# Expert stages of a two-block network: each token through its two chosen experts only, sorted by pair

## The reference, cut to what matters

```python
scores = jnp.einsum('bsd,de->bse', x, gate_w) + gate_b      # 4 experts
probs = jax.nn.softmax(scores, axis=-1)
topk_vals, topk_idx = jax.lax.top_k(probs, 2)
mask = jnp.sum(jax.nn.one_hot(topk_idx, 4), axis=-2)
masked = probs * mask
masked = masked / (jnp.sum(masked, axis=-1, keepdims=True) + 1e-09)
h = jax.nn.gelu(jnp.einsum('bsd,edh->ebsh', x, w1) + b1)    # 96 -> 384
y = jnp.einsum('ebsh,ehd->ebsd', h, w2) + b2                # 384 -> 96
out = jnp.einsum('bse,ebsd->bsd', masked, y)
...
t = t + _L0_ffn_ref(_ln_t(t), ...)
```

## Time and profile before

| what | value |
|---|---|
| median of three runs | 2661.78 us |
| span of the profiled execution | 2652.1 us |
| median less span | 9.7 us |
| stage 1 (to about 281 us) | 281 us |
| stage 2, experts (281 to 943) | 662 us |
| stage 3 (943 to 1989) | 1046 us |
| stage 4, experts (1989 to 2652) | 663 us |
| TensorE busy over the span | 89% |

### The profile page before, as it was taken

One profiled execution on the slowest core, in us unless ns is written; L12 is line 12 of the kernel. 1 busy time (PEld: TensorE's weight loads), 2 busy tenths in 40 slices (PEclk: granted clock), 3 DMA queues, 4 the chain that ended last, 5 costly groups with the idle time before them and its releaser, 6 DMA issues.

```text
span 2652.1 us, 72974 instructions
## 1 busy us (share of the span) xinstructions
PE 2365.9 (89%) x26354; PEld 1941.0 (73%) x26354; DVE 2112.4 (80%) x6729; ACT 1423.8 (54%) x2676; POOL 1125.1 (42%) x999
## 2 busy tenths in 40 slices
PE   3665799999999958999899989999968999999998
PEld 2554577777777747888787878888756777777776
DVE  4887788888888757888888878988857888888886
ACT  2332477777777634333333433333316777777776
POOL 1002244444444425555555545555533444444443
PEclk8777799999999978899998888988958999999999
DMA  6000000000000000000000000000000000000001
GB/s 120 1 0 0 16 1 0 0 0 0 0 0 0 1 18 3 3 3 2 4 2 3 2 3 3 2 3 2 3 2 1 0 24 0 0 24 0 24 0 24
DMA packets 39776, 19.48 MB, mean 7 GB/s; under 512 B 38146, under 2 KB 39332, under 8 KB 39560
## 3 DMA queue, kind: packets, MB, share of 16 engines
q1 hardware_dynamic: 39560, 16.43, 3.0%
HBM read 10.13 MB, written 6.29 MB: 6 GB/s over the span
## 4 chain that ended last, share of the span: by engine, by line
PE 63%; issue 19%; POOL 9%; DVE 8%; ACT 1%; POOLq 0%; DVEq 0%; ACTq 0%
PE ps L744 15%; PE ps L745 15%; PE ps L746 15%; PE ps L829 4%; PE ps L763 3%; POOL arena L506 3%; POOL arena L487 2%; PE ps L870 2%; PE ps L890 2%; PE ps L857 1%; PE ps L756 1%; PE ps L874 1%; POOL xn L498 1%; POOL arena L512 1%; DVE arena L939 1%
## 5 line engine op out<-in xcount | busy, mean ns | idle before, releaser
L442 POOL TENSOR_TENSOR rounded<-arena,rounded 128x512 fp32r<-128x512 f32 x384 | 497.2, 1295 | 729.2 <-ACT arena L578 729.2
L744 PE MATMUL ps<-rounded 128*96 128x512 f32 (+3 forms) x1856 | 728.3, 392 | 3.7 <-DVE rounded L366 3.0
L745 PE MATMUL ps<-rounded 128*96 128x512 f32 (+3 forms) x1856 | 698.6, 376 | 0.0
L746 PE MATMUL ps<-rounded 128*96 128x512 f32 (+3 forms) x1856 | 696.0, 376 | 0.0
L577 ACT ACTIVATE rounded<-ps 128x512 fp32r<-128x512 f32 x768 | 459.4, 598 | 317.3 <-PE ps L746 317.1
L578 ACT ACTIVATE arena<-ps 128x512 f32<-128x512 f32 x768 | 456.3, 594 | 0.0
L1203 DVE TENSOR_TENSOR rounded<-arena,rounded 128x512 fp32r<-128x512 f32 x384 | 278.4, 737 | 208.3 <-ACT arena L578 208.3
L829 PE MATMUL ps<-rounded 128*128 128x224 f32 (+1 forms) x2256 | 371.8, 309 | 40.8 <-ACT rounded L607 17.3
L746 PEld LDWEIGHTS ps<-rounded 128*96 128x96 f32 (+2 forms) x1856 | 331.0, 178 | 92.8
L745 PEld LDWEIGHTS ps<-rounded 128*96 128x96 f32 (+2 forms) x1856 | 335.6, 181 | 70.4 <-issue 0.2
L829 PEld LDWEIGHTS ps<-rounded 128*128 128x128 f32 x2256 | 324.2, 210 | 85.3 <-issue 31.7
(11 more groups left out here) (169 smaller groups left out, 3911.3 us busy)
## 6 DMA issues: line engine op xcount, KB each, us to landing
residual<-in_x SPq DMA_DIRECT2D x16, 384.0 KB, 6.3
out<-residual SPq DMA_DIRECT2D x16, 384.0 KB, 5.2
w<-in_w SPq DMA_DIRECT2D x4, 576.0 KB
arena<-in_W_conv SPq DMA_DIRECT2D x1, 756.0 KB
consts<-in_consts SPq DMA_DIRECT2D x1, 280.0 KB, 3.5
arena<-in_W2T SPq DMA_DIRECT2D x16, 4.0 KB
arena<-in_Win_x SPq DMA_DIRECT2D x1, 84.0 KB
arena<-in_Win_z SPq DMA_DIRECT2D x1, 72.0 KB
```

The costliest lines, as they stand in the source:

```text
L442: pool.tensor_tensor(hidr[:, 1, r, :], hid[:, r, :], hidr[:, 0, r, :].bitcast(F32), ALU.subtract).then_inc(f["low_pool"], 1)
L744: pe.matmul(dst, left[0], right[0], start=start, stop=False)
L745: pe.matmul(dst, left[1], right[0], start=False, stop=False)
L746: return pe.matmul(dst, left[0], right[1], start=False, stop=stop)
```

## The change

The expert stages are rewritten (`route` and `expert_tiles` in place of `ffn`), on all engines.

**Routing** (`route`), 4 groups of 4096 tokens. VectorE norms the rows into `stage`, whose row has 196 numbers: x, normed x, two weights, the token's number (`ROW`, `COL_GA`, `COL_GB`, `COL_ID`). ScalarE copies x there. TensorE transposes and computes the gate, plain float32. VectorE ranks, sets one of 6 pairs of experts for each token (`chosen`), TensorE counts the tokens before each one with two matmuls (`strict`, `every`), VectorE makes the slot (`placed`). GpSimd scatters each of 32 image rows with an indirect DMA, 128 rows of 784 bytes, into the DRAM tensor `rows`, where each pair has a region. After the last group VectorE makes a plan of the tiles (`planned`): TILES = (16384 + 6 x 511) // 512 = 37, each of one pair. SP pads the end of each region (`pads`).

**Tiles** (`expert_tiles`), 37 of 512 tokens, 6 chunks each, all unrolled. For each tile SP reads three numbers of the plan into registers (`value_load`) and issues three DMAs at addresses that depend on them: the token rows (512 x 784 bytes) and the split weights of two experts (each 128 x 5384 bytes, into `wring`, 2 slots). The result is added to the token rows in `xs`, and GpSimd scatters it with four indirect DMAs of 128 x 384 bytes: to the DRAM tensor `x1` in stage 2, to the output in stage 4.

**Around them.** The weights are split once, during stage 1, by GpSimd (`expert_parts`, 8 times) and written to DRAM (`wsp`). `xr` is read again from `x1` before stage 3. The output DMAs of SP are gone. Up has three banks in place of two, the lag is 4, GpSimd takes chunks 2 and 5, and the second bias is added by VectorE.

The diff, cut to its core:

```diff
-    def ffn(f, ln_before): ...                       # on each engine, 32 tiles x 12 chunks
+CPT = 2 * CPE
+LAG = 4
+XRING, HIDS, UPS = 6, 3, (0, 1, 5)
+ON_POOL = (2, 5)
...
+            # SP
+            def expert_tiles(l):
+                def tokens(t):
+                    if t >= TILES:
+                        return
+                    if t >= XRING:
+                        sp_.wait_ge(y_out[t % XRING], 16 * Q * uses(l, t - XRING, XRING))
+                    n = sp_.value_load(plan[0:1, 0, t:t + 1], min_val=0, max_val=NPAIR * REGION + (FILL - 1) * T512)
+                    sp_.dma_start(xs[:, t % XRING, :, :], rows[bass.ds(n, T512), :].rearrange("(p q) n -> p q n", q=Q)).then_inc(x_ld[t % XRING], 16)
+                def weights(t, e):
+                    if t >= 2:
+                        sp_.wait_ge(f["y_ev0" if e == 0 else "y_ev1"], l * TILES + t - 1)
+                    n = sp_.value_load(plan[0:1, 1 + e, t:t + 1], min_val=0, max_val=NEXP - 1)
+                    sp_.dma_start(wring[:, t % 2, e, :].bitcast(F32), wsp[l, bass.ds(n, 1), :, :].rearrange("o p n -> (o p) n")).then_inc(w_ld[t % 2][e], 16)
+                tokens(0)
+                for t in range(TILES):
+                    for e in range(2):
+                        weights(t, e)
+                    tokens(t + 1)
...
+            # GpSimd
+            def route(l):
+                def powers(g):
+                    pool.wait_ge(rt["var"], l * G + g + 1)
+                    pool.tensor_tensor(mom2[:, g % 2, 5, :], mom2[:, g % 2, 4, :], half_neg[:, :], ALU.pow).then_inc(rt["rstd"], 1)
+                def scatter(g):
+                    pool.wait_ge(rt["slots"], l * G + g + 1)
+                    pool.wait_ge(rt["copied"], l * G + g + 1)
+                    for h in range(SIDE):
+                        pool.indirect_dma_start(rows, bass.IndirectOffsetOnAxis(ap=slot[:, g % 2, h:h + 1], axis=0), stage[:, g % 2, h, :], None).then_inc(r_out[g % 2], 16)
...
+                powers(0)
+                for g in range(G):
+                    if g + 1 < G:
+                        powers(g + 1)
+                    scatter(g)
+            def expert_tiles(l):
...
+                for step in range(LAST + 3 * CPT):
+                    t, c = divmod(step, CPT)
+                    if c in ON_POOL and step < LAST:
+                        pool.wait_ge(f["gelu"], l * LAST + step + 1)
+                        if step >= CPT:
+                            pool.wait_ge(f["down"], l * LAST + step - CPT + 1)
+                        pool.tensor_tensor(hidr[:, 1, c, :], hid[:, step % HIDS, :], hidr[:, 0, c, :].bitcast(F32), ALU.subtract).then_inc(f["low_pool"], 1)
+                    if c in ON_POOL:
+                        scatter(t - 2, range(0, 2) if c == ON_POOL[0] else range(2, Q))
...
+            # TensorE
+                for step in range(LAST + LAG + 3):
+                    t, c = divmod(step, CPT)
+                    if step < LAST:
+                        up(step)
+                    if LAG <= step < LAST + LAG:
+                        down(step - LAG)
+                    if c == 2 and t + 1 < TILES:
+                        columns(t + 1)
+                    if (due := half_tile(step, LAG + 2)) is not None:
+                        y_rows(*due)
...
+            # VectorE
+            def route(l):
...
+                row_sums(0)
+                for g in range(G):
+                    normed(g)
+                    if g + 1 < G:
+                        row_sums(g + 1)
+                    gated(g)
+                    placed(g)
+                planned()
+            def expert_tiles(l):
...
+                for step in range(LAST + LAG + 4):
+                    t, c = divmod(step, CPT)
+                    if (due := half_tile(step, LAG + 1)) is not None and due[1] == 1:
+                        y_second(due[0])
+                    if (due := half_tile(step, LAG + 3)) is not None:
+                        combine(*due)
+                    if c == 4 and t + 1 < TILES:
+                        columns(t + 1)
+                    if step < LAST and c not in ON_POOL:
+                        dve.wait_ge(f["gelu"], l * LAST + step + 1)
+                        dve.tensor_tensor(hidr[:, 1, c, :], hid[:, step % HIDS, :], hidr[:, 0, c, :].bitcast(F32), ALU.subtract).then_inc(f["low"], 1)
```

More of the change, by code:

```diff
@@ L271, in bank, with uses, half_tile @@
             return ps[:, b:b + n, :].rearrange("p a b -> p (a b)")
[L273 to L279, removed]
+        def uses(l, t, ring):
+            return l * len(range(t % ring, TILES, ring)) + t // ring + 1
+        def half_tile(step, lag):
+            t, e = divmod(step - lag - (CPE - 1), CPT)
+            if e % CPE == 0 and 0 <= t < TILES:
+                return t, e // CPE
+            return None
+        LAST = CPT * TILES
         def layer_norm(dve, ch, src, dst, n, width, which_eps, count, ready, part=None, own=None, rows=None):
@@ new lines, in _ @@
+            sp_.wait_ge(b2_set, 1)
+            for l in range(2):
+                with nc.allow_non_contiguous_dma(reason="biases, one element to a partition"):
+                    sp_.dma_start(b2[0:D, l, :, 0:1], inp["ffn"][l]["b2T"].rearrange("d (e o) -> d e o", o=1)).then_inc(rc_in, 16)
+                sp_.dma_start(gw[0:D, l, :], inp["ffn"][l]["gate_w"]).then_inc(rc_in, 16)
+                sp_.dma_start(gw[D:D + 1, l, :], inp["ffn"][l]["gate_b"]).then_inc(rc_in, 16)
+            raw_weights(0)
@@ new lines, in gates, with expert_tiles, columns @@
+            def gates(l, g, k):
+                pe.wait_ge(rt["xt"], (l * G + g) * NQ + k + 1)
+                if k == 0 and (g or l):
+                    pe.wait_ge(rt["gates"], l * G + g)
+                for i in range(Q):
+                    at_col = (Q * k + i) * NEXP
+                    ins = pe.matmul(bank(5)[:, at_col:at_col + NEXP], xt[0:D + 1, k % 2, i * P:(i + 1) * P], gw[0:D + 1, l, :], start=True, stop=True)
+                ins.then_inc(rt["gate_pe"], 1)
+            def expert_tiles(l):
+                def columns(t):
+                    pe.wait_ge(x_ld[t % XRING], 16 * uses(l, t, XRING))
+                    need(pe, f["x_lo"], l * TILES + t)
@@ L800, in ffn @@
-                pe.wait_ge(f["parts"], 1)
-                tiles(pe, tile)
+                        need(pe, f["y_ev0" if e == 0 else "y_ev1"], l * TILES + t)
+                    mine = [x for x in range(CPT) if (x in ON_POOL) == (c in ON_POOL)]
+                    pe.wait_ge(f["low_pool" if c in ON_POOL else "low"], (l * TILES + t) * len(mine) + mine.index(c) + 1)
+                    w = wring[:, t % 2, e, W1COLS:W1COLS + W2COLS].rearrange("p (s c d) -> p s c d", s=2, d=D)
+                    product(bank(2 + e)[0:D, :], halves(w[:, :, n, :]), halves(hidr[:, :, c, :]), n == 0, n == CPE - 1).then_inc(f["down"], 1)
```

678 lines of the change are left out of this document (421 added, 257 removed).

## The result

The changed kernel took 2714.41 us (median of 4 runs, 2712.84 to 2725.24) beside 2660.92 us before: the ratio is 1.0213, with a 95% interval from 1.0188 to 1.0237. It is slower, clear of the interval; whether by more than 2% the interval leaves open. The forecast was 2579 us and faster.

The account below looks back on a forecast made before the run. TensorE was taken to bound the expert stages, 1324 us. Two stages of 443 + 132X plus a 12 us reload give 898 + 264X, 1241 at X = 1.3: -83, span 2569, median 2579 us; 8-in-10 range 2430 to 2790.

Parts of the forecast that it names:

- A group is 32X + 5.4: Routing: GpSimd's 32 indirect DMAs plus one 5.4 us power set a group's time, binding from X = 0.7 on.
- X: GpSimd's time for one indirect DMA: taken as 1.3 us, ends kept 0.32 and 2.65, break-even 1.61.
- Products: Expert tiles: 222 chunks in place of 384; TensorE takes 9.4 us a tile, 349 us for 37.
- SP's loop: Expert tiles: weights wait for the tile before last, tokens queue behind; at least 10.2 us a tile, taken as 10.0, 370 us.
- Routing, where increments are on time: All work in front of a stage's first product: 61 + 128X, with about 40 us to the first group's slots.
- two round trips: Routing's first group: VectorE's small operations with two round trips to TensorE, together 13 us.
- The ends: Each expert stage: drain 6, slow clock at the start 3, last scatter 4X + 3 us.
- The reload: Between the stages: group 0 of x is read again before stage 3, 12 us, once.
- Rival 1: Indirect DMAs dear, issued serially on GpSimd: 2808 us at X = 2.0, 3173 at 2.65; chance 0.17.
- Rival 2: SP's loop is longer: at 12 us a tile +148, 2727 us; chance 0.13.
- Rival 3: VectorE binds the routing, with X under 1.0: 2405 us at X = 0.32; chance 0.13.
- Rival 4: VectorE's operations hold up GpSimd's issues of indirect DMAs; chance 0.10.

Follow-up runs that it names:

- both: Changed kernel with tokens loaded two tiles ahead and one semaphore increment for a group's 32 statistics: 2550.32 us, 0.96 of before.
- powers_early: Changed kernel with tokens two tiles ahead, one increment per group's statistics, and GpSimd's powers of three groups before its first scatter: 2540.65 us, 0.9574 of before.
- unchanged: The changed kernel run again on another chip, nothing edited: 2606.99 us, 0.9815 of before.
- paced: Changed kernel with each indirect DMA of the routing waiting for the one before to land: 2972.99 us, 1.1178 of before; repeated, 2966.84.
- plain_dma: Changed kernel with SP's plain in-order DMAs in place of the routing's indirect ones, so another output: 2505.12 us, 0.9436 of before; repeated, 2508.11.
- mixed: Changed kernel with plain DMAs in the first routing; in the second, indirect DMAs back to back, one at a time, or in bursts of four: 2639.07 us, 0.9926.
- warm: Like powers_early, plus 8 TensorE products at the start of each routing to raise its clock: 2664.22 us, 1.0026 of before.
- unchanged_3: The changed kernel run a fourth time, nothing edited, on the chip that also ran warm: 2725.74 us, 1.0246 of before.
- one_inc: Changed kernel with one semaphore increment for a group's 32 row statistics instead of 32: 2607.95 us, 0.9811 of before; repeated, 2611.05.

## Why the prediction was wrong, point by point

**The step that failed on the measured chip.** "A group is 32X + 5.4", with VectorE's 28 us of the next group under the scatter: the overlap was taken as free. A group measured 62.2, 63.6 and 61.2 us in place of 46, since the chain of TensorE, ScalarE and VectorE under the scatter all but stood still for most of it. That this is what turned the sign is shown by the same program on both kinds of chip. Spans 2723.4 and 2604.4: of 119.0 us, the routings make 285.4 - 232.0 = 53.4 and 287.3 - 231.8 = 55.5; stage 3 makes 9.4, in which no increment is late and which I can't explain (its length also differs by 15 us between both and powers_early). By medians, 2607.0, 2607.6 and 2607.0 on three chips make the kernel 1.9 to 2.0% faster than before, inside the forecast's own range of 2500 to 2660; 2714.4 and 2725.7 in two measurements on the other kind make it 2.1 and 2.5% slower. The prediction had no term for a difference between chips, so which sign it met was chance.

**Products.** Right. With the tokens early a tile takes 9.48 us, where I had 9.4 for TensorE alone.

**SP's loop.** The mechanism was right, the size small: 10.46 us a tile in place of 10.0. TensorE's waits for SP's load over 250 us of tiles, unchanged kernel, and those of SP:

```profile
PE ps L964 <- DMA arena<-rows: 16.4, 24, 1.0
```

```profile
SPq L495 <- DVE arena L1481: 134.7, 24, 5.9
SPq L495 <- ACT arena L751: 37.2, 25, 1.6
```

SP waits as foretold for the second expert of the tile before last (L1481), and the tokens behind it reach TensorE 0.7 us late in each tile. Early tokens end that: 2559 against 2607. I had worked out 10.2 and taken 10.0; the working was the better number.

**Routing, where increments are on time.** 232.0 us against 227.4. The first scatter came at 49 us and not 40: 3.2 us for the tables' DMA, and 7.0 until TensorE, at a granted clock of 0.50 with 2.43 us for each of 8 quads, had the scores. I had counted "two round trips" in 13 us and no work of TensorE's. Of these 9.3 us, X took back 3.0 (the four scatters with the powers between them lasted 174.2 us for 177.2) and the way to the first product 1.5 (8.5 us for 10).

**X.** 1.27 us, and I took 1.3 as the 128x512 operation's. That an indirect DMA needs a few words for each row, which made me take that one, was my estimate; no run shows it. Its place in the sum is shown by paced: the spacing went from 1.27 to 2.74 us (124 steps in 340.0 us in stage 4), and 256 x 1.47 = 376 us are to be compared with 2972.99 - 2606.99 = 366.

**The ends.** From the first product to the start of stage 3 409.3 us for my 399.2, in stage 4 402.0 for 387.2. The reload, 18.7 us from VectorE's last addition to its first operation of stage 3, is what I had for the last scatter and the load (8.2 + 12):

```profile
902.75 0.99 DVE L1489 SCALAR_TENSOR_TENSOR arena<-ps,arena 128x96 f32<-128x96 f32 x4 [0.64 <-PE ps L992]
922.44 0.17 DVE L1129 TENSOR_SCALAR arena<-arena 128x12 f32<-128x12 f32 x1 [18.70 <-DMA residual<-after_ffn]
```

The rest is the tiles and, in stage 4, eight indirect DMAs after the last addition and not four. On these chips the parts add up to -83 + 35 = -48 us of span, as measured (2604.4 - 2652.1).

**The rivals.** Rival 1 (dear indirect DMAs) was priced by its issue alone; the issue was cheap (1.27 us). Rival 2 was half a microsecond a tile. Rival 3 shows its floor in plain_dma: with nothing for GpSimd to issue a group takes 33 us, not VectorE's 28, since VectorE waits for the scores there as well (6.90 us in the third group). Rival 4, that VectorE's operations hold up GpSimd's issues, had a single row for it, a 4-element operation of VectorE's that took 1.31 us beside GpSimd's of 1.30; no row had a DMA issued by GpSimd. It predicts longer issues beside VectorE, and small ones are there. In unchanged 19 of the 248 issues that aren't a group's first took 1.02 to 1.40 us, every one beside an operation of VectorE's on two inputs:

```profile
352.18 1.40 POOL L571 DMA_INDIRECT rows<-arena  x1 [0.30 <-issue]
352.66 0.69 DVE L1387 TENSOR_TENSOR arena<-arena 128x512 f32<-128x512 f32 x1
```

Together they cost about 1.4 us a routing, where three scatters that each wait for VectorE's 28 us would make 84; beside VectorE's scalings (L1369) no issue took over 0.97. The longest of all runs is one of 1.94 us in the tiles of powers_early, so no run shows an issue held for the length of VectorE's work. The dear end of this rival, on which the upper end of the range leaned, was my estimate, and no run shows it. I had looked for the engines in GpSimd's way and not for GpSimd in theirs. No rival had the mechanism that came.

**What stays open.** Why some chips do this and others not. The kernel before takes 2655 to 2661 us on all, and which chip the first measurement had is not recorded. One more thing goes with the slow kind: records of increments are lost there, those of landings too. Of the 512 increments at the landings of the first group's indirect DMAs 75 have a record in the first measurement, and 512 in unchanged, though the last is as prompt (371.62 us, 2.2 us after the last issue began). So theory P, that the recording itself makes the delay, is an untested rival; the record has no run that is known to be without it. Whether the stall is one of carrying out increments or of something in front of that was not told apart either.

## What to carry to other kernels

Price a transfer by what it does to the others while it runs, not only by its issue: a trace that has none of a kind (here indirect DMAs by GpSimd) says nothing of that, and such a change wants a range and a rival for it. Where work of other engines must run beside many indirect DMAs, keep few of them under way at once: in mixed 4 of 8 copies came late beside 32 back to back, by up to 31.7 us, and none of 8 beside bursts of four. Passing fewer semaphores was no cure in the one kernel where it could be seen (warm, 24 late copies with it and 24 without in unchanged_3). When a trace shows events late, see whether their records are missing, and believe only the delays that a wait bears out. Before a fix is believed, run the unchanged kernel next to it: one_inc seemed to gain 106 us and gained none.

## What the runs showed of the hardware

In the first measurement and on two further chips (the first's may be one of them), work of TensorE, ScalarE and VectorE was held up beside indirect DMAs that GpSimd issued every 1.27 us, 32 in a row: up to 32.5 us passed from the end of TensorE's transposes to ScalarE's copy of them, which took 0.04 us in unchanged, and the records of the increments that ended these waits are as late. On three other chips none of some 8400 increments in any kernel came over 0.1 us late, and the longest such gap was 0.5 us. A version with tokens two tiles ahead, one increment per group and the early powers took 2540.65 us, 4.3% below before, on a chip of the fast kind; nearly the same version (warm) was 0.3% above before on one of the slow kind. An indirect DMA of 128 rows of 784 bytes took GpSimd 0.96 us and 0.30 of issue, and landed 2.4 us after it began (median in unchanged; 2.3 to 4.8).
